# For the last batch's four rows, VectorE finishes the second fp4 rounding itself; GpSimd keeps only the block normalisation

## The reference

```python
def fp4_quant_dequant(x):
    xb = x.reshape(shape[:-1] + (shape[-1] // BLOCK, BLOCK))
    scale = jnp.max(jnp.abs(xb), axis=-1, keepdims=True) / 6.0
    scale = jnp.maximum(scale, jnp.float32(1e-12))
    xn = xb / scale
    idx = jnp.searchsorted(_MID, jnp.abs(xn))
    q = _GRID[idx] * jnp.sign(xn) * scale
...
gate = fp4_linear(x, w_gate)      # 128 -> 352
y = fp4_linear(x, w_up)           # 128 -> 352
h = jax.nn.silu(gate) * y
return fp4_linear(h, w_down)      # 352 -> 128
```

## Time and profile before

| what | before |
|---|---|
| median of 3 runs | 421.15 us (420.87 to 424.14) |
| profiled execution, its own time | 423.29 us |
| profiled execution, span from first to last instruction | 421.6 us |
| VectorE busy in the span | 299.5 us, 71% |
| TensorE busy in the span | 298.0 us, 71% |
| GpSimd busy in the span | 192.8 us, 46% |
| mean granted TensorE clock | 0.784 of full |

### The profile page before, as it was taken

The page is one execution under the profiler, slowest core; times in us unless marked ns, Lnnn a source line. Parts: engine busy times, 40 slices in busy tenths (PEclk is TensorE's granted clock), DMA queues, the critical chain, the costliest instruction groups (busy, mean ns, idle before and its releaser), DMA issues.

```text
span 421.6 us, 6515 instructions
## 1 busy us (share of the span) xinstructions
PE 298.0 (71%) x1790; PEld 144.2 (34%) x1790; DVE 299.5 (71%) x1137; ACT 177.5 (42%) x327; POOL 192.8 (46%) x374
## 2 busy tenths in 40 slices
PE   1684678757877768868785979787797664848553
PEld 1272332212234123334432434334243323536332
DVE  5467656446647576898879787899977536677882
ACT  5351355543546354445454435355545412322111
POOL 4214207322306363363757553545545535563653
PEclk9998555756768686889888588899979968665696
DMA  8069000260300052004002600040000000000000
GB/s 214 27 198 178 1 0 4 75 151 0 78 0 1 24 174 32 1 0 83 2 8 75 158 1 8 2 83 7 3 6 3 7 0 8 7 0 9 1 12 19
DMA packets 20835, 17.50 MB, mean 42 GB/s; under 512 B 1920, under 2 KB 20224, under 8 KB 20800
## 3 DMA queue, kind: packets, MB, share of 16 engines
q1 hardware_dynamic: 20272, 16.50, 16.0%
q10 hardware_dynamic: 528, 0.59, 0.5%
HBM read 9.62 MB, written 7.34 MB: 40 GB/s over the span
## 4 chain that ended last, share of the span: by engine, by line
PE 39%; DVE 30%; issue 11%; POOL 8%; DMA 6%; ACT 4%; SPq 1%; DVEq 0%; POOLq 0%; ACTq 0%
PE pvp L1116 9%; DVE summed L832 8%; PE mxp L1081 5%; PE st L1105 4%; DMA ks<-parts_dram 3%; PE mxp L1015 3%; PE misc L1195 3%; PE misc L1180 2%; DMA parts_dram<-parts 2%; DVE space L768 2%; POOL space L476 2%; DVE stats L737 2%; PE misc L1177 2%; DVE space L748 2%; DVE space L765 2%
## 5 line engine op out<-in xcount | busy, mean ns | idle before, releaser
L832 DVE CUSTOM_DVE_ANT_0 summed<-mxp,causal 128x512 bf16<-128x512 f32 (+3 forms) x256 | 114.0, 486 | 19.8 <-PE mxp L1081 19.3
L633 ACT ACTIVATE probs<-st 128x1024 f32<-128x1024 f32 (+1 forms) x96 | 84.6, 881 | 85.4 <-PE st L1105 85.1
L1081 PE MATMUL mxp<-ks,qs 48*128 48x512 bf16 (+3 forms) x256 | 40.8, 357 | 49.1 <-DVE rmax L832 37.9
L1116 PE MATMUL pvp<-probs,va 128*32 128x128 f32 (+3 forms) x512 | 60.4, 558 | 5.1 <-POOL probs L446 5.1
L446 POOL TENSOR_SCALAR_AFFINE_SELECT probs<-probs 128x256 f32<-128x256 f32 x128 | 48.0, 411 | 23.0 <-ACT probs L633 23.0
L543 ACT ACTIVATE space<-misc 128x128 f32<-128x128 f32 (+3 forms) x78 | 24.2, 327 | 48.5 <-PE misc L1136 18.2
L1105 PE MATMUL st<-qs,ks 50*128 50x512 bf16 (+3 forms) x256 | 41.4, 363 | 3.5 <-ACT probs L633 2.2
L1081 PEld LDWEIGHTS mxp<-ks,qs 48*128 48x128 bf16 x256 | 11.9, 98 | 69.4 <-DVE rmax L832 42.5
L476 POOL TENSOR_TENSOR space<-space 128x128 f32<-128x128 f32 (+2 forms) x33 | 24.8, 752 | 23.6 <-DVE space L771 23.6
L463 POOL TENSOR_TENSOR space<-space,xrden 128x256 f32<-128x256 f32 x16 | 9.8, 615 | 40.9 <-DVE xrden L889 40.9
L488 POOL TENSOR_TENSOR space<-space,reciph 128x352 f32<-128x352 f32 x16 | 12.6, 785 | 32.3 <-DVE reciph L759 32.3
(11 more groups left out here) (196 smaller groups left out, 593.9 us busy)
## 6 DMA issues: line engine op xcount, KB each, us to landing
parts_dram<-parts SPq DMA_DIRECT2D x8, 384.0 KB, 2.6
qs<-parts_dram SPq DMA_DIRECT2D x16, 192.0 KB, 3.8
ks<-parts_dram SPq DMA_DIRECT2D x16, 192.0 KB, 4.4
parts_dram<-parts SPq DMA_DIRECT2D x8, 256.0 KB, 2.9
xin<-in_x SPq DMA_DIRECT2D x4, 256.0 KB, 8.2
parts_dram<-parts SPq DMA_DIRECT2D x8, 128.0 KB, 2.9
out<-outr SPq DMA_DIRECT2D x16, 64.0 KB, 1.6
qs<-nrows SPq DMA_DIRECT2D x32, 4.0 KB
```

The source lines that it names most:

```text
L633: nc.scalar.activation(probs[n % 2][:, 2 * pair:2 * pair + 2, 512 * k:512 * k + w], st2[:, :].rearrange("p (h q) -> p h q", h=2)[:, :, 0:w ...
L832: last = v.tensor_tensor_reduce(out=summed[:, m % 2, e * w:(e + 1) * w], in0=mxp[m % 3][:, e * w:(e + 1) * w], in1=causal[:, S - w:S], sca ...
L1081: last = mm(units[r][:, e * w:(e + 1) * w], qs[rows, c, i * P:(i + 1) * P], ks[rows, c, 0:w], start=True, stop=True)
L1116: last = mm(pvp[32 * i:32 * i + 32, j * P:S], va[:, j, GH * (n % NG) + i, :], probs[n % 2][:, i, OFF[j]:OFF[j] + S - P * j], start=(j == 0 ...
```

## The change

`finish_fp4` for the second rounding is no longer issued on GpSimd for rows 12 to 15. In its place VectorE, right behind its three rounding steps of such a row, issues the same subtract and the same multiply, each behind a wait on its predecessor. Two new semaphores, `roundh_last` and `dqh_last`, count them, and TensorE's transposes of these rows wait for `dqh_last`. Nothing else is moved; GpSimd keeps L488 for all rows, and rows 0 to 11 are as before.

```diff
@@ in gpsimd stage_c
-                if u == 9:
+                if u == 9 and k < LAST:
                     finish_fp4(tanh[:, r, :], gated[:, r, :], scaleh[:, r, :], hid[:, r, :], "sumh_d", "roundh_d",
                                "dqh_d", k)
@@ in vector stage_c
                 if u == 8:
 
                     round_fp4(tanh[:, r, :], gated[:, r, :], "normh_d", "exph_d", "clamph_d", "sumh_d", k)
+                    if k >= LAST:
+                        wait(dve, "sumh_d", k + 1)
+                        v.tensor_tensor(tanh[:, r, :], tanh[:, r, :], gated[:, r, :], ALU.subtract)\
+                            .then_inc(s["roundh_last"], 1)
+                        wait(dve, "roundh_last", k - LAST + 1)
+                        v.tensor_tensor(blocks(hid[:, r, :]), blocks(tanh[:, r, :]), spread(scaleh[:, r, :], BLK),
+                                        ALU.mult).then_inc(s["dqh_last"], 1)
@@ in tensor stage_d
                 if u == 1:
-                    pe.wait_ge(s["dqh_d"], k + 1)
+                    if k < LAST:
+                        pe.wait_ge(s["dqh_d"], k + 1)
+                    else:
+                        pe.wait_ge(s["dqh_last"], k - LAST + 1)
```

More of the change, by code:

```diff
@@ L259, in decoder_layer @@
             dqxT_mm dqxT_d gate_mm tanh_d gated_d up_mm hid_d maxh_d scaleh_d reciph_d normh_d clamph_d exph_d
-            sumh_d roundh_d dqh_d dqhT_mm dqhT_d down_mm outr_d""".split()
+            sumh_d roundh_d dqh_d roundh_last dqh_last dqhT_mm dqhT_d down_mm outr_d""".split()
         s = {n: sem(n) for n in names}
```

## The result

| what | before | changed |
|---|---|---|
| median of 20 runs, first comparison | 422.13 us (415.75 to 430.64) | 425.87 us (421.48 to 429.96) |
| ratio of that comparison, 95% interval | | 1.0127 (1.0093 to 1.0162) |
| difference of the means of all its runs | | +3.7 us, +/- 1.8 |
| four comparisons together (113 and 56 runs), mean | 422.57 us | 424.40 us, so +1.83 +/- 0.87 (ratio 1.0043) |
| profiled execution, span | 421.6 us | 420.6 us |

A forecast was written before the change was run, and what follows sets the result against it. In the last rows VectorE's and GpSimd's paths run side by side, nearly equally long. Three rounds +2.70 and tail -0.72 give +1.98; 421.15 + 2.0 = 423.2 us, range 421.2 to 425.6.

The forecast's parts named there:

- The round: L765 of one late row to L765 of the next: from 3.93 to 4.83 us, three rounds, +2.70 us.
- The tail: Last L765 to TensorE's start on row 15: from 3.21 to 2.49 us, so -0.72.
- The sum: Rounds plus tail, 2.70 - 0.72 = +1.98 us, all between 400.93 and TensorE's last transposes.
- How the numbers follow: Whole kernel's time: difference added to the median of the runs shown, 421.15 + 2.0 = 423.2 us.
- rival A: TensorE's clock falls early, in the stretched rounds, delaying row 14's L765: +0.6 more, total +2.6, 423.8 us; chance 0.10.
- Rival B: TensorE's clock is up in the tail, giving back 1.14 us: total +0.8, 422.0 us; chance 0.11.
- Rival C: Faster engine wins: late rows handed to TensorE 0.72 us sooner, four rows save 2.9 us, 418.3 us; chance 0.03.
- D: The new VectorE pair costs GpSimd's prices, 0.94 and 0.78: +4.6 us, 425.7 us; chance 0.06.
- the low bound: New VectorE operations take 0.34 us each: round +0.54, total +0.5, 421.7 us; chance 0.06 shared with E.
- E: Nothing measurable: tail gain and rounds cancel, needing rounds longer by only 0.24 us; chance 0.06 shared with the low bound.
- The shared time with GpSimd: VectorE and GpSimd waiting for each other in the late rounds: charged nothing, at most 0.79 us per round.

The follow-up runs named there:

- (5): Changed kernel, but for rows 12 to 15 VectorE does the subtract and GpSimd the multiply; 424.06 us median of 12 runs, ratio 0.9987.
- (4): Changed kernel with two more VectorE subtracts of 128x352 between subtract and multiply in each of the last four rows; 428.69 us, ratio 1.0154.
- (7): Kernel before with row 15 alone finished on VectorE, plus idle transposes on TensorE; 422.01 us median of 6 runs, ratio 0.989.
- fourth trace: The changed kernel measured a fourth time, no edit; 424.42 us median of 12 runs, ratio 1.0094 against the kernel before.
- experiment 10: Kernel before with rows 12 to 14 alone finished on VectorE, row 15 on GpSimd; its one run took 422.06 us.
- pair later: Changed kernel with the subtract and multiply issued on VectorE behind the next row's reciprocal (L759); 424.41 us, ratio 1.0052.
- row 15 with idle work, again: Same kernel measured a second time: row 15 alone on VectorE plus idle TensorE transposes; 421.51 us median of 12 runs, ratio 1.0001.
- experiment 3: Kernel before with row 15 alone finished on VectorE, rows 12 to 14 on GpSimd; 422.55 us, ratio 0.9972.
- experiment 6: Changed kernel with the pair of row k issued on VectorE behind L759 of row k+1, ahead of L913 of row k+2; 424.41 us, ratio 1.0052.

## Why the prediction was right and where it was wrong

**The round.** Forecast 4.83, measured 4.80 to 4.83 in every round of that order in which VectorE did not wait for TensorE. The price of the new operations (0.53) was that of the neighbours in the earlier trace rows. The step that carried it, that the pair stands on VectorE ahead of the next row's reciprocal and so ahead of L488, was tested from three sides: one operation there costs 0.33 a round (5), two 0.90 (the changed kernel), four 2.00 (4). Each of these is 0.56 per operation less some 0.23: that much of VectorE's longer path was hidden under GpSimd's L476 and L478, and all of the rest is paid.

**The tail.** Forecast 2.49, measured 2.45. With row 15 alone at the old rounds it is 2.46 and the stretch 14.26, 0.74 under before (7). So the change has two halves of opposite sign: for the row that has no next row VectorE is the better place, for the three that have one GpSimd is, since there its work was free.

**The sum.** Forecast +1.98, traces +1.91 in three of four, and +1.83 +/- 0.87 in the times of the four comparisons together. VectorE's busy time from the first L765 to the end is 14.89 against 10.80 us, +4.1 (forecast 4.2); GpSimd's 2.36 against 9.09, -6.7 (forecast -6.9). That the mean of all times falls so near to the forecast is in part luck, as the four comparisons run from -0.1 to +3.7.

**The step that failed** is the last one of its sum, from the difference to the time ("How the numbers follow"): the base of 421.15 to which +2.0 was added, and the width of the range. The terms of the difference held. First, 421.15 was the median of three runs; over 20 it was 422.13, over all 113 it was 422.8. That is 1.0 of the 2.7 us between 423.2 and 425.87. Second, the upper end was to lie above rival A by as much as the median lies below the profiled execution. That is 2.1 us, and 423.8 + 2.1 is 425.9; the 425.6 that was written is 0.3 less, and 425.87 falls in between. But the distance of one execution from the median of three is no measure of the scatter. The 113 runs of before have a standard deviation of 3.0 us, so a mean of 20 runs is good to 1.3 us and the difference of two such means to 1.8, which the range should have held beside its mechanisms. The means of the first comparison differed by 3.7, of which the stretch accounts for 1.9. The cause of the other 1.8 stays open. It is not a cost of the change that comes each time (-0.1, +1.1 and +1.8 in all, against 1.9 from the stretch), no instruction in the untouched part differs between the kernels, and the changed kernel's four traces reach row 12 no later than before's. But chance from run to run alone doesn't explain it well either, as said above, and what shifts between sets of runs was not found.

**Rival A** was taken as something that the change would cause, with a chance of 0.10 and a price of 0.6. The price was right (0.65 to 0.67 in the fourth trace and in experiment 10). The reason is not shown. A mostly halved clock in the middle round (granted 0.50 to 0.62) came in six of the fourteen traces. In "two more subtracts" the round was long enough to hide it; in the other five VectorE waited (changed, fourth; row 15 only; rows 12 to 14; pair later; row 15 with idle work, again). Two of the five have the old rounds up to there, and the instructions up to there are those of before. In the fourth trace and in rows 12 to 14 the clock was at 0.50 already in the first round, ahead of anything that longer rounds could do. So it can come without the change, and there it costs more, since the old rounds have less slack for TensorE: 12.62 - 11.79 = 0.83 for the three rounds in experiment 3. None of the three traces with all rows on GpSimd had it, though. The third round is less even: there the clock was 0.50 or 0.51 in five of the six traces with rounds of 4.8 us or more, and below 0.9 in two of the six with the old rounds. That fits rival A's reason, but TensorE had slack there and the half clock cost nothing in the longer rounds. Fourteen traces are too few to say whether the change makes it more frequent.

**Rival B** came in part in one of the four traces of the changed kernel. In the second the clock was still full for the last transposes, and 5.31 us lie behind the stretch instead of 5.6:

```profile
416.39 0.55 PE L1198 MATMUL mxp<-ident,space 128*128 128x128 f32 x3 [2.64 <-DVE space L931]
```

That is 0.3 of the 1.1 us that B would give back; the last down matmuls take 1.62 in all four. Less than 5.3 us lie behind the stretch only where TensorE was given idle work. **Rival C** falls with the three rounds, **D** and the low bound with the 0.53, **E** with a round that grew by 0.90 where it wanted 0.24. **The shared time with GpSimd** was rightly charged at nothing for this order; experiment 6 shows what it costs when the pair does run beside L488, 0.45 us on the multiply and 0.15 on L488, less than the 0.79 that was named as the most.

## What to carry to other kernels

Before moving work from a slow engine to a faster one, list what stands behind it on the fast engine's queue, and ask which of it the slow engine waits for: here 1.7 us of GpSimd work was free because VectorE needed that time for the next row, and 1.1 us of VectorE work in its place cost 0.9 a round. The last element of a pipeline has no next one, and the answer there may be the opposite. Where an effect is below the scatter of single runs, compare the stretch it touches in several traces, repeat the comparison of times on another occasion, and take the range of a forecast from the scatter of the runs as well as from the mechanisms.

## What the runs showed of the hardware

The same instructions, in the same order, reach row 12's first L765 anywhere between 394.43 and 402.55 us in the fourteen traces, while an undisturbed round repeats to 0.03 us. TensorE's granted clock ahead of that point differs between traces. The fastest and the slowest to reach it, in this order (from:to, length, TensorE busy and count, granted clock):

```profile
340.00:390.00 50.00, 29.12 (x135) 0.80 0.02 5
```

```profile
340.00:390.00 50.00, 32.36 (x144) 0.70 0.02 5
```

The two stretches are the same times and not the same instructions. That the clock is the whole cause of the 8 us was not tried.

With idle transposes into an unused bank TensorE's clock was full through the tail in two traces and through part of it in a third (behind the stretch 4.51, 4.57 and 4.99 us, 5.31 to 5.67 in the eleven traces without them). In one of the two it had been at half in the middle round, ahead of the first idle transposes, and came back to full in the third.
